# A recurrent layer on one core: half of the odd step's update goes from VectorE to GpSimd, silu is made in one ScalarE instruction, gates by tanh, a shorter layer norm

## The chip, the cores and the metric

One Trainium2 chip; the program uses one of its cores. The metric is the device time in microseconds (us), from one launch to its end; lower is better. All arithmetic is fp32.

## The reference, cut to what matters

x has 8 sequences of 2048 tokens of 512 features. Each token is normalised twice (a plain layer norm `xn`, and a second one with gain and bias inside the layer), goes through a depthwise convolution of three taps along time, and then through matrix products:

```python
x_norm = _layernorm(xn, ln_in_g, ln_in_b)
x_norm = x_norm + conv(x_norm) + conv_b
gate, input_gate = split(x_norm @ gate_w.T + gate_b)
gate = sigmoid(gate)
Bm = x_norm * sigmoid(input_gate) @ B_w.T + B_b
Cm = x_norm @ C_w.T + C_b
A_bar = expm(dt_A * A)                      # 64 x 64
def step(state, bc):                        # 2048 times, state is 8 x 64
    b_t, c_t = bc
    s = _layernorm(state @ A_bar + b_t, ln_st_g, ln_st_b)
    return (s, c_t * s)
ssm = ys @ D_w.T + D_b
out = x + (ssm * gate) * silu(xn @ W.T + b + (xn @ V_r) @ C.T)
```

The scan of 2048 dependent steps on a state of 8 x 64, with a layer norm in each, is what can't be done in parallel.

## The kernel before, in words

**Chunks.** Time is cut into 32 chunks (`NC`) of 64 steps (`CT`). One iteration i of the main loop runs the 64 scan steps of chunk i ("F"), prepares chunk i+1 (layer norm, transposes, convolution, input gate, B and C products: "A"), computes the layer norm statistics of x two chunks ahead ("S"), and finishes chunk i-1 (y, the output product, gating, adding x, storing: "C"). The order on each engine is written out by hand: tables of numbers say behind which scan step t (0 to 63) each piece of side work stands (`V_CONV`, `V_SILU`, `V_SG`, `V_STATS`, `V_XG`, `V_ADD`, `V_G` for VectorE, `PE_...` for TensorE, `POOL_LN` for GpSimd). ScalarE has no scan work; its order is in `iteration` of its block.

**The scan.** Tile `dw` holds, for each of the 8 sequences (partitions) and each step t, a slot of columns: r (`CR`, one), a constant (`CE`), w (`CD` to `CM`, 64), a (`CM` to `CM2`, 64) and a third block (`CM2` to `SLOT`, 64). w is the centred, not yet scaled state; r is 1 over its standard deviation. Steps come in pairs:

- even step (`even_step`): VectorE makes w of t as r(t-1) times a of t-1, added to the slot's w (L727, 64 wide); takes its sum of squares (`square_sum`, L717, into q); then, with the product that TensorE has made from the w of the pair before (`look_ahead`, L990 and L991, in `scanP`), makes a and the third block of t (L731, 128 wide).
- odd step (`odd_step`): VectorE makes w and a of t in one instruction from a and the third block of t-1, scaled by r(t-1) (L740, 128 wide: `CD:CM2` from `CM:SLOT`); takes the sum of squares; transposes w for TensorE (L744).
- behind each sum of squares GpSimd raises q to the power -1/2 and writes r (`step`, L356), and the next step of VectorE waits for it (semaphore `r_ready`).

So a step is: VectorE update, VectorE sum of squares, GpSimd power, and round again. Side work on VectorE stands behind the step's own instructions, while GpSimd makes the power.

**Around it.** silu is made of a sigmoid by ScalarE (`ffn_sigmoid`, L493, tile `sigf`) and two half-wide multiplications by VectorE (`silu`, L679). The input gate (L465) and the output gate (L498) are sigmoids in place in PSUM, each followed by a VectorE product (L673, L686). The layer norm of x is 16 small GpSimd instructions (`ln_op`, L375 to L390): mean negated, variance plus eps, four powers (one column each) for r1, three to get the variance after the first norm, four powers for r2, three products. Each waits for the one before by a semaphore. They stand between the scan's powers, and three groups of them run ahead of the loop. SyncE issues all transfers, x of the next chunks among them (`prefetch_xa`, L246).

Of the kernel before, what the change touches and what calls it, by code (L numbers as in the profile page):

```python
# [13 lines left out]
P = 128  # L14
B = 8
# [63 lines left out]
POOL_LN = (43, 43, 44, 45, 46, 47, 48, 48, 49, 50, 51, 52, 53, 54, 54, 55)  # L79
# [17 lines left out]
def build(nc, x, ident_d, gateT_d, WT_d, VT_d, CrT_d, BT_d, CwT_d, DT_d, vec_d, small_d, Bb_d, out):  # L97
    with ExitStack() as ctx:
# [36 lines left out]
        ln = sb("ln", [P, 8, NJ])  # L135
# [52 lines left out]
        def released(user, i):  # L188
# [157 lines left out]
        def _(pool):  # L346
# [11 lines left out]

            def ln_op(n, k):

                mean, var = mv[:, :, 0], mv[:, :, 1]
                nm, a, r1, v2, r2, rr, bx, bz = (ln[:, a, :] for a in range(8))
# [5 lines left out]
                if k == LN_OPS - 3:  # L368
# [7 lines left out]
                    lambda: g.tensor_scalar(a, var, EPS, None, ALU.add),  # L376
                    lambda: half_power(a, r1, 0),
# [768 lines left out]
```

## Time and profile before

| | |
|---|---|
| median of 3 runs | 2668.4 us (2668.17 to 2672.42) |
| the profiled execution, its own time | 2673.4 us |
| its span in the profile | 2671.6 us |
| VectorE busy | 2163.5 us, 81% |
| GpSimd busy | 1305.1 us, 49% |
| TensorE busy (matmul) | 2510.1 us, 94% |
| ScalarE busy | 826.4 us, 31% |
| granted TensorE clock, mean | 0.991 |

Busy time is the share of the span in which an engine had an instruction under way; the chain of waits follows the work that ended last backwards through whatever released it. The 1.8 us between the profiled execution's time and its span lie outside the span.

### The profile page before, as it was taken

To read this page: it belongs to the slowest core of one execution; us is meant where nothing else is said; L and a number is where in the kernel's file an instruction comes from. 1 tells how busy PE (TensorE), PEld (TensorE's weight loads), DVE (VectorE), ACT (ScalarE), POOL (GpSimd) and SP (SyncE) were. 2 spreads that over 40 slices of the span, in tenths; PEclk is the share of its full clock that TensorE was granted. 3 is DMA by queue.
4 is the path that set the end of the run, shared out by engine and by line. 5 is a ranking of instruction groups with operands and counts; after the bars stand their busy time and mean duration, and the time that the engine had idled before them with its cause. 6 is when DMAs were issued, how large, how long until landed. Compare 5 with 4: busy or idle time off the path is not lost.

```text
span 2671.6 us, 39956 instructions
## 1 busy us (share of the span) xinstructions
PE 2510.1 (94%) x9999; PEld 1303.0 (49%) x9999; DVE 2163.5 (81%) x9732; ACT 826.4 (31%) x1354; POOL 1305.1 (49%) x2584
## 2 busy tenths in 40 slices
PE   2899999999999999999999999999999999999985
PEld 1445555555455555545555545555554555555543
DVE  3478888888888888888888888888888888888875
ACT  0423333322333322333332233332233333223310
POOL 3154455555455555445555545555544555554442
PEclk9999999999999999999999999999999999999997
DMA  2001122112112211211211211221121121121112
GB/s 88 23 22 50 45 51 56 40 38 56 45 47 55 56 39 39 52 45 50 56 42 39 53 47 44 56 56 40 38 54 45 48 56 47 37 50 47 32 36 49
DMA packets 99835, 125.03 MB, mean 47 GB/s; under 512 B 32231, under 2 KB 48807, under 8 KB 99608
## 3 DMA queue, kind: packets, MB, share of 16 engines
q1 hardware_dynamic: 99608, 122.48, 18.3%
q8 instruction: 85, 1.39, 0.2%
q14 instruction: 142, 1.16, 0.1%
HBM read 71.92 MB, written 33.55 MB: 39 GB/s over the span
## 4 chain that ended last, share of the span: by engine, by line
DVE 50%; POOL 34%; issue 12%; PE 3%; POOLq 0%; SPq 0%; ACT 0%; DMA 0%; DVEq 0%; ACTq 0%
POOL dw L356 27%; DVE wq L717 13%; DVE dw L740 11%; DVE dw L727 7%; POOL ln L373 5%; DVE wT L744 4%; DVE bank L658 3%; DVE xnorm L664 3%; DVE sgT L703 3%; DVE xg L673 3%; DVE o L711 1%; DVE G L686 1%; PE bank L957 1%; DVE ys L694 1%; PE bank L897 0%
## 5 line engine op out<-in xcount | busy, mean ns | idle before, releaser
L356 POOL TENSOR_TENSOR dw<-q,minus_half 8x1 f32<-8x1 f32 x2048 | 1105.5, 540 | 1239.7 <-DVE wq L717 1228.3
L990 PEld LDWEIGHTS bank<-Mscan,wT 128*65 128x65 f32 x2046 | 215.8, 136 | 760.1 <-issue 755.3
L740 DVE SCALAR_TENSOR_TENSOR dw<-dw 8x128 f32<-8x128 f32 x1024 | 347.7, 340 | 207.7 <-POOL dw L356 191.1
L957 PE MATMUL bank<-xnorm,gateT 128*128 128x512 f32 x1024 | 508.6, 600 | 0.9 <-issue 0.9
L948 PE MATMUL bank<-xnorm,gateT 128*128 128x512 f32 x1024 | 504.4, 594 | 0.0
L717 DVE SCALAR_TENSOR_TENSOR wq<-dw 8x65 f32<-8x65 f32 x2048 | 443.4, 217 | 70.3
L940 PE MATMUL bank<-xnT,WT 128*128 128x512 f32 x1024 | 494.9, 594 | 0.0
L990 PE MATMUL bank<-Mscan,wT 128*65 128x128 f32 x2046 | 409.9, 282 | 86.6 <-DVE wT L744 36.1
L991 PE MATMUL bank<-Mscan,wT 128*65 128x128 f32 x2046 | 393.0, 274 | 0.0
L727 DVE SCALAR_TENSOR_TENSOR dw<-dw 8x64 f32<-8x64 f32 x1024 | 271.4, 265 | 132.5 <-POOL dw L356 125.6
L731 DVE SCALAR_TENSOR_TENSOR dw<-bank,dw 8x128 f32<-8x128 f32 x1024 | 342.6, 335 | 8.2 <-PE bank L991 7.8
L465 ACT ACTIVATE bank<-bank,vec 128x512 f32<-128x512 f32 x128 | 84.8, 662 | 618.6 <-PE bank L957 618.6
L991 PEld LDWEIGHTS bank<-Mscan,wT 128*65 128x65 f32 x2046 | 254.3, 139 | 0.2
L744 DVE STREAM_TRANSPOSE wT<-dw 32x64 f32<-32x64 f32 x1024 | 232.8, 227 | 0.0
L940 PEld LDWEIGHTS bank<-xnT,WT 128*128 128x128 f32 x1024 | 167.5, 191 | 95.3 <-issue 95.3
L957 PEld LDWEIGHTS bank<-xnorm,gateT 128*128 128x128 f32 x1024 | 161.4, 192 | 90.5 <-issue 89.9
L948 PEld LDWEIGHTS bank<-xnorm,gateT 128*128 128x128 f32 x1024 | 171.1, 191 | 62.1 <-issue 62.1
L498 ACT ACTIVATE bank<-bank,vec 128x512 f32<-128x512 f32 x128 | 84.7, 662 | 374.6 <-PE bank L948 374.6
L493 ACT ACTIVATE sigf<-bank,vec 128x512 f32<-128x512 f32 x128 | 87.6, 684 | 215.1 <-PE bank L940 211.2
L717 DVE DVE_READ_ACCUMULATOR wq<-dw 8x1 f32 x2048 | 145.3, 71 | 0.0
L373 POOL TENSOR_TENSOR ln<-ln,minus_half 128x1 f32<-128x1 f32 x264 | 142.8, 541 | 4.3 <-POOL ln L373 3.2
L920 PE MATMUL bank<-ident,sgT 128*128 128x128 f32 x512 | 141.0, 280 | 1.4 <-DVE sgT L703 0.8
(136 smaller groups left out, 2511.1 us busy)
## 6 DMA issues: line engine op xcount, KB each, us to landing
xa<-in_x SPq DMA_DIRECT2D x256, 128.0 KB, 2.7
xc<-in_x SPq DMA_DIRECT2D x256, 128.0 KB, 2.7
out<-o SPq DMA_DIRECT2D x256, 128.0 KB, 2.3
dw<-dtok SPq DMA_DIRECT2D x128, 96.0 KB
wtok<-dw SPq DMA_DIRECT2D x128, 33.0 KB
gateT<-in_gateT SPq DMA_DIRECT2D x1, 2048.0 KB
WT<-in_WT SPq DMA_DIRECT2D x1, 1024.0 KB, 9.0
xc<-in_x SPq DMA_DIRECT2D x8, 124.0 KB
```

The lines of the kernel that those rows point to most:

```text
L356: nc.gpsimd.tensor_tensor(dw[0:B, t, CR:CR + 1], q[:], minus_half[0:B, 0:1], ALU.pow).then_inc(s["r_ready"], 1)
L373: half_power = lambda a, b, j: g.tensor_tensor(col(b, j), col(a, j), minus_half[:, j:j + 1], ALU.pow)
L717: V.scalar_tensor_tensor(out=wq[:], in0=w_eps, scalar=1.0 / S, in1=w_eps, op0=ALU.mult, op1=ALU.mult, accum_out=q[:]).then_inc(s["q_ready" ...
L727: V.scalar_tensor_tensor(out=dw[0:B, t, CD:CM], in0=dw[0:B, before, CM:CM2], scalar=r, in1=dw[0:B, t, CD:CM], op0=ALU.mult, op1=ALU.add).t ...
L731: V.scalar_tensor_tensor(out=dw[0:B, t, CM:SLOT], in0=scanP[0:B, 0:2 * S], scalar=r, in1=dw[0:B, t, CM:SLOT], op0=ALU.mult, op1=ALU.add).t ...
L740: V.scalar_tensor_tensor(out=dw[0:B, t, CD:CM2], in0=dw[0:B, before, CM:SLOT], scalar=dw[0:B, before, CR:CR + 1], in1=dw[0:B, t, CD:CM2], ...
L744: V.transpose(wT[0:32, 0:S], dw[:, t, CD:CM]).then_inc(s["wT_ready"], 1)
L940: ins = mm(mbank["ffn", m][:], WT[:, k, P * m:P * m + P], xnT[:, k, :], start=(k == 0), stop=(k == KH - 1))
L948: ins = mm(mbank["gate", m][:], gateT[:, k, P * m:P * m + P], xnorm[p][:, k, :], start=(k == 0), stop=(k == KH - 1))
L957: ins = mm(mbank["ig", m][:], gateT[:, k, H + P * m:H + P * m + P], xnorm[p][:, k, :], start=(k == 0), stop=(k == KH - 1))
L990: mm(scanP[0:WIDE, 0:2 * S], wT[:, 0:WIDE], Mscan[:, 0, :], start=True, stop=False)
L991: mm(scanP[0:WIDE, 0:2 * S], wT[:, 32:32 + WIDE], Mscan[:, 1, :], start=False, stop=True).then_inc(s["p_ready"], 1)
```

## The change

1. **The odd step's a goes to GpSimd.** VectorE's odd update is 64 wide now (w alone). GpSimd gets `next_a` ahead of the odd step's power: a multiplication by r(t-1) into a new tile `scaled` (`tensor_scalar`, 8x64) and an addition (`tensor_tensor`, 8x64). The first waits for `r_ready` and `rest_ready`, the second for the first (`a_scaled`). The even step on VectorE waits for `a_ready` too.
2. **silu and gates.** ScalarE makes silu in one instruction straight into `G`; VectorE's eight half-wide products per chunk go. Both gates are tanh of half the argument, and VectorE's products become (tanh + 1) times the other operand; the factors of one half go into `C_b`, `ys`, `BT` and the gates' biases in the setup.
3. **Layer norm.** r1 times r2 is the power -1/2 of var * (1 + EPS) + EPS * EPS, so 13 instructions take the place of 16.
4. **Places.** The statistics stand at t = 18 to 32 instead of 26 to 40, their aggregation at 34 instead of 42, GpSimd's layer norm at 35 to 53 instead of 43 to 55.

```diff
-V_SILU = (6, 8, 12, 14, 16, 18, 20, 22)
-V_STATS = (26, 28, 30, 32, 34, 36, 38, 40)
-V_AGGR = 42
+V_STATS = (18, 20, 22, 24, 26, 28, 30, 32)
+V_AGGR = 34
-POOL_LN = (43, 43, 44, 45, 46, 47, 48, 48, 49, 50, 51, 52, 53, 54, 54, 55)
+POOL_LN = (35, 35, 35, 37, 39, 41, 43, 45, 47, 49, 51, 53, 53)
...
+            def next_a(i, t):
+                here, before = dw[0:B, t, CM:CM2], dw[0:B, t - 1, CM2:SLOT]
+                wait_for(pool, "r_ready", CT, i, t)
+                wait_for(pool, "rest_ready", PAIRS, i, t // 2 + 1)
+                nc.gpsimd.tensor_scalar(scaled[:], before, dw[0:B, t - 1, CR:CR + 1], None,
+                                        ALU.mult).then_inc(s["a_scaled"], 1)
+                wait_for(pool, "a_scaled", PAIRS, i, t // 2 + 1)
+                nc.gpsimd.tensor_tensor(here, scaled[:], here, ALU.add).then_inc(s["a_ready"], 1)
+
             def step(i, t):
+                if t % 2:
+                    next_a(i, t)
                 wait_for(pool, "q_ready", CT, i, t + 1)
...
+                    lambda: g.tensor_scalar(both, var, 1.0 + EPS, EPS * EPS, ALU.mult, ALU.add),
                     lambda: half_power(a, r1, 0),
...
-                    lambda: g.tensor_tensor(v2, var, r1, ALU.mult),
-                    lambda: g.tensor_tensor(v2, v2, r1, ALU.mult),
-                    lambda: g.tensor_scalar(a, v2, EPS, None, ALU.add),
-                    lambda: half_power(a, r2, 0),
...
-                    lambda: g.tensor_tensor(rr, r1, r2, ALU.mult),
+                    lambda: half_power(both, rr, 0),
...
-                a_(mbank["ig", m][:], mbank["ig", m][:], ACT.Sigmoid,
+                a_(mbank["ig", m][:], mbank["ig", m][:], ACT.Tanh, scale=0.5,
...
-            def ffn_sigmoid(c, m):
-                wait_for(act, "silu_done", 2 * KH, c, 2 * m - 2)
-                a_(sigf[:, m % 2, :], mbank["ffn", m][:], ACT.Sigmoid,
-                   bias=v_("ffn_b", m)).then_inc(s["sig_done"], 1)
+            def ffn_silu(c, m, p):
+                if m == 0:
+                    wait_for(act, "sg_done", KH, c - 1, 0)
+                a_(G[p][:, m, :], mbank["ffn", m][:], ACT.Silu, bias=v_("ffn_b", m)).then_inc(s["silu_done"], 1)
...
-                V.tensor_tensor(xg[:, m, :], mbank["ig", m][:], xnorm[p][:, m, :],
-                                ALU.mult).then_inc(s["xg_done"], 1)
-            def silu(c, m, h, p):
-                V.scalar_tensor_tensor(out=G[p][:, m, part], in0=mbank["ffn", m][:, part], scalar=v_("ffn_b", m),
-                                       in1=sigf[:, m % 2, part], op0=ALU.add, op1=ALU.mult
+                V.scalar_tensor_tensor(out=xg[:, m, :], in0=mbank["ig", m][:], scalar=1.0, in1=xnorm[p][:, m, :],
+                                       op0=ALU.add, op1=ALU.mult).then_inc(s["xg_done"], 1)
...
                 wait_for(dve, "r_ready", CT, i, t)
+                wait_for(dve, "a_ready", PAIRS, i, t // 2)
                 V.scalar_tensor_tensor(out=dw[0:B, t, CD:CM], in0=dw[0:B, before, CM:CM2], scalar=r,
...
-                V.scalar_tensor_tensor(out=dw[0:B, t, CD:CM2], in0=dw[0:B, before, CM:SLOT],
-                                       scalar=dw[0:B, before, CR:CR + 1], in1=dw[0:B, t, CD:CM2],
+                V.scalar_tensor_tensor(out=dw[0:B, t, CD:CM], in0=dw[0:B, before, CM:CM2],
+                                       scalar=dw[0:B, before, CR:CR + 1], in1=dw[0:B, t, CD:CM],
...
+            link(V.tensor_scalar(vec[:, gates, :], vec[:, gates, :], 0.5, None, ALU.mult))
+            link(V.tensor_scalar(sm("C_b"), sm("C_b"), 0.5, None, ALU.mult))
```

What stands in a row on GpSimd before, from the start of the loop to the middle of chunk 0 (L356 is the power of a step, L375, L376 and L373 are the first layer norm instructions, behind steps 43 to 45):

```order
L356 TENSOR_TENSOR dw<-q,minus_half 8x1 [waits q_ready] x44
L375 TENSOR_SCALAR ln<-mv 128x4 [waits mv_done,xn_done]
L376 TENSOR_SCALAR ln<-mv 128x4 [waits ln_done]
L356 TENSOR_TENSOR dw<-q,minus_half 8x1 [waits q_ready]
L373 TENSOR_TENSOR ln<-ln,minus_half 128x1 [waits ln_done]
```

And after the change, steps 33 to 38 of a chunk (L367 is the power now, L358 and L361 the two new instructions, L386 to L388 the first three of the layer norm, L384 one of its powers):

```order
L358 TENSOR_SCALAR scaled<-dw 8x64 [waits rest_ready,r_ready]
L361 TENSOR_TENSOR dw<-scaled,dw 8x64 [waits a_scaled]
L367 TENSOR_TENSOR dw<-q,minus_half 8x1 [waits q_ready]
L386 TENSOR_SCALAR ln<-mv 128x4 [waits mv_done,xn_done]
L387 TENSOR_SCALAR ln<-mv 128x4 [waits ln_done]
L388 TENSOR_SCALAR ln<-mv 128x4 [waits ln_done]
L367 TENSOR_TENSOR dw<-q,minus_half 8x1 [waits q_ready]
L358 TENSOR_SCALAR scaled<-dw 8x64 [waits rest_ready,r_ready]
L361 TENSOR_TENSOR dw<-scaled,dw 8x64 [waits a_scaled]
L367 TENSOR_TENSOR dw<-q,minus_half 8x1 [waits q_ready]
L384 TENSOR_TENSOR ln<-ln,minus_half 128x1 [waits ln_done]
```

Between an even step's power and the odd step's power there now stand two instructions, of which the first waits for the even power itself and the second for the first; between an odd power and the next even one stands nothing new but the layer norm's pieces, three of them behind step 35.

VectorE before, steps 26 and 27 with the side work between them (L727 even update, L740 odd update, L717 sum of squares, L744 transpose, L638 statistics):

```order
L727 SCALAR_TENSOR_TENSOR dw<-dw 8x64 [waits r_ready]
L717 SCALAR_TENSOR_TENSOR wq,q<-dw 8x65 [waits w_ready]
L731 SCALAR_TENSOR_TENSOR dw<-bank,dw 8x128 [waits p_ready]
L638 BN_STATS stats<-xa 128x6 [waits xa_in]
L740 SCALAR_TENSOR_TENSOR dw<-dw 8x128 [waits rest_ready,r_ready]
L717 SCALAR_TENSOR_TENSOR wq,q<-dw 8x65 [waits w_ready]
L744 STREAM_TRANSPOSE wT<-dw 32x64
```

VectorE after, a pair of steps with the same kinds of side work (L728 even update, L741 odd update, L645 statistics, L745 transpose):

```order
L728 SCALAR_TENSOR_TENSOR dw<-dw 8x64 [waits a_ready,r_ready]
L717 SCALAR_TENSOR_TENSOR wq,q<-dw 8x65 [waits w_ready]
L732 SCALAR_TENSOR_TENSOR dw<-bank,dw 8x128 [waits p_ready]
L645 BN_STATS stats<-xa 128x6
L741 SCALAR_TENSOR_TENSOR dw<-dw 8x64 [waits rest_ready,r_ready]
L717 SCALAR_TENSOR_TENSOR wq,q<-dw 8x65 [waits w_ready]
L745 STREAM_TRANSPOSE wT<-dw 32x64
```

The odd update has become 64 wide, the even one waits for `a_ready` as well, and the rest stands as it did, less the L679 products that stood behind eight of the even steps.

## Rows read from the trace of the kernel before

**Rows 1.** The page, the chain of waits: shares of the span by engine, then by line.

```profile
DVE 50%; POOL 34%; issue 12%; PE 3%; POOLq 0%; SPq 0%; ACT 0%; DMA 0%; DVEq 0%; ACTq 0%
POOL dw L356 27%; DVE wq L717 13%; DVE dw L740 11%; DVE dw L727 7%; POOL ln L373 5%; DVE wT L744 4%; DVE bank L658 3%; DVE xnorm L664 3%; DVE sgT L703 3%; DVE xg L673 3%; DVE o L711 1%; DVE G L686 1%; PE bank L957 1%; DVE ys L694 1%; PE bank L897 0%
```

**Rows 2.** Timeline, chunk 14: start us, duration us, engine, line, operation [idle before <-releaser].

```profile
1302.00 0.54 POOL L356 TENSOR_TENSOR dw<-q,minus_half 8x1 f32<-8x1 f32 x1 [0.65 <-DVE wq L717]
...
1302.57 0.34 DVE L740 SCALAR_TENSOR_TENSOR dw<-dw 8x128 f32<-8x128 f32 x1 [0.39 <-POOL dw L356]
1302.94 0.22 DVE L717 SCALAR_TENSOR_TENSOR wq<-dw 8x65 f32<-8x65 f32 x1
...
1303.25 0.54 POOL L356 TENSOR_TENSOR dw<-q,minus_half 8x1 f32<-8x1 f32 x1 [0.71 <-DVE wq L717]
...
1303.82 0.27 DVE L727 SCALAR_TENSOR_TENSOR dw<-dw 8x64 f32<-8x64 f32 x1 [0.50 <-POOL dw L356]
...
1304.43 0.54 POOL L356 TENSOR_TENSOR dw<-q,minus_half 8x1 f32<-8x1 f32 x1 [0.65 <-DVE wq L717]
```

**Rows 3.** Timeline of GpSimd: the scan's first power and, 2047 powers on, its last.

```profile
124.12 0.54 POOL L356 TENSOR_TENSOR dw<-q,minus_half 8x1 f32<-8x1 f32 x1 [9.04 <-DVE wq L717]
...
2648.88 0.54 POOL L356 TENSOR_TENSOR dw<-q,minus_half 8x1 f32<-8x1 f32 x1 [0.74 <-DVE wq L717]
```

**Rows 4.** Timeline of VectorE, chunk 0: the longest wait of the scan for TensorE.

```profile
129.05 0.34 DVE L731 SCALAR_TENSOR_TENSOR dw<-bank,dw 8x128 f32<-8x128 f32 x1 [2.58 <-PE bank L991]
```

**Rows 5.** GpSimd, groups of the whole span: count | busy us, mean ns | idle before.

```profile
L348 POOL MEMSET dw<- 32x12416 f32 x1 | 10.4, 10435 | 0.0
L375 POOL TENSOR_SCALAR ln<-mv 128x4 f32<-128x4 f32 x33 | 8.0, 243 | 79.4 <-issue 41.3 <-DVE mv L650 35.6
...
L383 POOL TENSOR_SCALAR ln<-ln 128x4 f32<-128x4 f32 x33 | 7.3, 220 | 0.6 <-POOL ln L382 0.6
L382 POOL TENSOR_TENSOR ln<-ln 128x4 f32<-128x4 f32 x33 | 6.6, 201 | 5.9 <-POOL ln L381 5.9
...
L351 POOL MEMSET dw<- 8x64 f32 x1 | 0.2, 208 | 0.0
...
L350 POOL MEMSET dw<- 8x1 f32 x1 | 0.1, 89 | 0.1
```

**Rows 6.** Timeline of GpSimd, layer norm ahead of the loop, each waiting for the last.

```profile
56.93 0.20 POOL L382 TENSOR_TENSOR ln<-ln 128x4 f32<-128x4 f32 x1 [0.18 <-POOL ln L381]
57.33 0.23 POOL L383 TENSOR_SCALAR ln<-ln 128x4 f32<-128x4 f32 x1 [0.20 <-POOL ln L382]
57.74 0.57 POOL L373 TENSOR_TENSOR ln<-ln,minus_half 128x1 f32<-128x1 f32 x1 [0.18 <-POOL ln L383]
```

**Rows 7.** Timeline of GpSimd, chunk 14: a power of the layer norm behind one of the scan.

```profile
1288.55 0.54 POOL L356 TENSOR_TENSOR dw<-q,minus_half 8x1 f32<-8x1 f32 x1 [0.20 <-DVE wq L717]
1289.07 0.54 POOL L373 TENSOR_TENSOR ln<-ln,minus_half 128x1 f32<-128x1 f32 x1
```

**Rows 8.** VectorE, groups of the whole span.

```profile
L740 DVE SCALAR_TENSOR_TENSOR dw<-dw 8x128 f32<-8x128 f32 x1024 | 347.7, 340 | 207.7 <-POOL dw L356 191.1
...
L727 DVE SCALAR_TENSOR_TENSOR dw<-dw 8x64 f32<-8x64 f32 x1024 | 271.4, 265 | 132.5 <-POOL dw L356 125.6 <-DMA dw<-dtok 6.9
...
L679 DVE SCALAR_TENSOR_TENSOR G<-bank,vec,sigf 128x256 f32<-128x256 f32 x256 | 118.4, 463 | 0.0
```

**Rows 9.** Stretch, busy us (count) of PE, PEld, DVE, ACT, POOL, clock, DMA share, GB/s.

```profile
1230.00:1309.00 79.00, 77.03 (x312) 40.00 (x311) 66.68 (x302) 25.78 (x44) 40.21 (x80) 1.00 0.19 48
```

**Rows 10.** ScalarE: its one table load of the span.

```profile
L515 ACT ACT_TABLE_LOAD x1 | 1.3, 1283 | 0.7 <-PEq L1136 0.7
```

**Rows 11.** Timeline of SyncE, chunk 14: the eight transfers of x for the statistics.

```profile
1242.88 4.95 SPq L246 DMA_DIRECT2D xa<-in_x  x8
```

**Rows 12.** The page, DMA issues: KB each, median us from issue to landing.

```profile
xa<-in_x SPq DMA_DIRECT2D x256, 128.0 KB, 2.7
```

**Rows 13.** Timeline of GpSimd, chunk 14: the power of step 18.

```profile
1253.03 0.54 POOL L356 TENSOR_TENSOR dw<-q,minus_half 8x1 f32<-8x1 f32 x1 [0.70 <-DVE wq L717]
```

More of the change, by code:

```diff
@@ L361, in ln_op @@
                 mean, var = mv[:, :, 0], mv[:, :, 1]
-                nm, a, r1, v2, r2, rr, bx, bz = (ln[:, a, :] for a in range(8))
+                nm, a, r1, both, rr, bx, bz = (ln[:, a, :] for a in range(7))
                 if k == 0:
@@ L380, in ln_op @@
                     lambda: half_power(a, r1, 3),
-                    lambda: g.tensor_tensor(v2, var, r1, ALU.mult),
-                    lambda: g.tensor_tensor(v2, v2, r1, ALU.mult),
-                    lambda: g.tensor_scalar(a, v2, EPS, None, ALU.add),
-                    lambda: half_power(a, r2, 0),
-                    lambda: half_power(a, r2, 1),
-                    lambda: half_power(a, r2, 2),
-                    lambda: half_power(a, r2, 3),
-                    lambda: g.tensor_tensor(rr, r1, r2, ALU.mult),
+                    lambda: half_power(both, rr, 0),
+                    lambda: half_power(both, rr, 1),
+                    lambda: half_power(both, rr, 2),
+                    lambda: half_power(both, rr, 3),
                     lambda: g.tensor_tensor(bx, nm, r1, ALU.mult),
@@ L672, in gated_x @@
                     wait_for(dve, "xnorm_done", KH, c, KH)
-                V.tensor_tensor(xg[:, m, :], mbank["ig", m][:], xnorm[p][:, m, :],
-                                ALU.mult).then_inc(s["xg_done"], 1)
-            def silu(c, m, h, p):
-                wait_for(dve, "sig_done", KH, c, m + 1)
-                part = slice(TOK // 2 * h, TOK // 2 * (h + 1))
-                V.scalar_tensor_tensor(out=G[p][:, m, part], in0=mbank["ffn", m][:, part], scalar=v_("ffn_b", m),
-                                       in1=sigf[:, m % 2, part], op0=ALU.add, op1=ALU.mult
-                                       ).then_inc(s["silu_done"], 1)
+                V.scalar_tensor_tensor(out=xg[:, m, :], in0=mbank["ig", m][:], scalar=1.0, in1=xnorm[p][:, m, :],
+                                       op0=ALU.add, op1=ALU.mult).then_inc(s["xg_done"], 1)
             def whole_gate(c, m, p):
                 wait_for(dve, "gates_done", KH, c, m + 1)
-                wait_for(dve, "silu_done", 2 * KH, c, 2 * m + 2)
-                V.tensor_tensor(G[p][:, m, :], mbank["gate", m][:], G[p][:, m, :],
-                                ALU.mult).then_inc(s["g_done"], 1)
+                wait_for(dve, "silu_done", KH, c, m + 1)
+                V.scalar_tensor_tensor(out=G[p][:, m, :], in0=mbank["gate", m][:], scalar=1.0, in1=G[p][:, m, :],
+                                       op0=ALU.add, op1=ALU.mult).then_inc(s["g_done"], 1)
             def state_times_c(c, p):
@@ L794, in _ @@
                         if n == 1:
-                            ins = V.tensor_scalar(btmp[:], btmp[:], -1.0 / S, None, ALU.mult)
+                            ins = V.tensor_scalar(btmp[:], btmp[:], -0.5 / S, None, ALU.mult)
                         else:
-                            ins = V.tensor_tensor(BT[:, :, 0:S], BT[:, :, 0:S], btmp[:].unsqueeze(2).to_broadcast([P, KH, S]),
-                                                  ALU.add)
+                            ins = V.scalar_tensor_tensor(out=BT[:, :, 0:S], in0=BT[:, :, 0:S], scalar=0.5,
+                                                         in1=btmp[:].unsqueeze(2).to_broadcast([P, KH, S]),
+                                                         op0=ALU.mult, op1=ALU.add)
                     ins.then_inc(s["bt_steps"], 1)
@@ L866, in iteration @@
                     if F:
-                        if t in V_SILU:
-                            silu(i, *divmod(V_SILU.index(t), 2), p)
                         if t in gate_at:
@@ L1101, in _ @@
             iteration(NC, 0, "C", False)
-LN_OPS = 16
-SETUP_VEC = 1
+LN_OPS = 13
+SETUP_VEC = 3
 SETUP_SERIES = SETUP_VEC + 11
```

45 lines of the change are left out of this document (23 added, 22 removed).

## The prediction

> **What bounds the kernel now.** I read the chain of waits first. VectorE has 50% of it and GpSimd 34% [rows 1], and the lines are those of the scan: the power, the sum of squares, the two updates. So the question is not which engine is busiest but how long one round is. The timeline of a calm stretch shows it [rows 2]. A power starts at 1302.00 and takes 0.54; the odd update starts at 1302.57, the sum of squares at 1302.94, the next power at 1303.25: 1.25 us from the even power to the odd one. From there the even update starts at 1303.82 and the next power at 1304.43: 1.18 us. The reader should see that the odd step is 0.07 longer for one reason: its update is 128 wide, 340 ns against 265 ns [rows 8]. In both, VectorE is idle until the power is done (0.39 and 0.50 before the updates).
>
> The first and the last of the 2048 powers are 2524.76 us apart [rows 3]. One wait of 2.58 us for TensorE at the start of chunk 0 is a single event [rows 4]; without it, a pair of steps takes 2 x (2524.76 - 2.58) / 2047 = **2.464 us**, against 1.25 + 1.18 = 2.43 in the calm stretch. The whole kernel is 1024 such pairs, 124 us ahead of them and some 23 behind. VectorE's side work hides in the power's shadow and costs the other 0.03. Hence every 0.01 us in a pair is 10.2 us of time.
>
> **The change, part by part.** *The new path on GpSimd.* Between the even power and the odd one there were 1.25 us, all VectorE's. Now two ways have to be through before the odd power starts, and the longer decides.
>
> VectorE's way: the update is 64 wide as in the even step, so 1.18 us.
>
> GpSimd's way, from the start of the even power: 0.54 for the power; then the multiplication, which waits for that power's result by a semaphore on the same engine; then the addition, which waits for the multiplication; then the power, which does not wait for the addition. What an instruction pays that waits for the one before it on GpSimd is in the layer norm ahead of the loop [rows 6]: 0.20 ahead of a tensor_scalar, 0.18 ahead of a tensor_tensor. One that doesn't wait starts 0.02 before the end of the last (1288.55 to 1289.07 is 0.52 for a power of 0.54) [rows 7]. The way is therefore L = 0.54 + 0.20 + m + 0.18 + s - 0.02 = 0.90 + m + s, with m and s the times of the two instructions.
>
> No row has these on 64 elements. With 4 elements a tensor_scalar takes 0.22 and a tensor_tensor 0.20 [rows 5]. For 60 elements more, the fills give two rates [rows 5]: the large one 10.4 us / 12416 = 0.84 ns per element, the small one on the very shape 8x64 (208 - 89) / 63 = 1.9 ns, though that one is strided. At 0.84 it is m = 0.27, s = 0.25; at 1.9, m = 0.33, s = 0.31; and if each of the addition's two inputs costs 1.9, s = 0.43. I take s = 0.31, since the addition reads two inputs and the fill none, and m = 0.30, between its two ends: its operand is contiguous, but its factor comes from memory, while the factors of the rows are constants. So **L = 1.51**, with ends 1.42 and 1.66. GpSimd's way is longer than VectorE's by 0.33.
>
> The Trainium skill speaks against this move: "GPSIMD Engine Reference", section "Engine selection", gives elementwise adds and multiplies to VectorE, with GpSimd about two times slower on two inputs and at about line rate on one. By its figures (one element per cycle at 1.2 GHz for the multiplication, 4497 ns for 2048 elements for the addition) I estimate m at 0.27 and s at 0.33, and the total would be 10 us less than mine; no row here shows either on 64 elements.
>
> *The gap from the odd power to the even one* stays 1.18. The even update waits for `a_ready` too, but the addition is over before the odd power starts. A second satisfied wait costs nothing: the odd update had two and starts 0.57 behind the power, as the even one does with one [rows 2]. Side work behind odd steps no longer runs over, because VectorE now gets there L - 1.18 = 0.33 before GpSimd starts the power. A pair is 1.51 + 1.18 = 2.69, and 1024 x (2.69 - 2.464) = **+231 us**.
>
> *The layer norm's start.* Behind step 35 stand three dependent tensor_scalars: from the start of the power 0.52, then three of about 0.24 with two gaps of some 0.19, less 0.02: 1.60 instead of 1.18 [rows 5 to 7]. In 30 chunks that is **+12 us**. The other places hold one power, 0.52 + 0.54 = 1.06, or two products, about 1.10, both under 1.18.
>
> *Ahead of the loop.* The layer norm there loses four instructions of some 0.4 from start to start [rows 6] and gains one, -1.1; two more small VectorE instructions in the setup, at about half a microsecond together, +0.5. **-0.6 us**.
>
> *Costed at nothing.* The removed silu products, 256 x 463 ns = 118 us of VectorE [rows 8], lay in the shadow of the even power and ran over it by a few hundredths; that gain is in the 2.464, and it can't appear while GpSimd is later. The same goes for the 75 ns of the narrower update. ScalarE's silu and tanh: it is busy 25.8 of 79 us in a chunk [rows 9]; were silu and tanh in different tables, two loads of 1.28 [rows 10] per chunk would still fit, and the list of instructions holds one load, as before. The gate products with a constant added lie behind odd steps, with 0.33 us more cover than before. The statistics at step 18: x is issued by 1247.83, lands some 2.7 later at 1250.5, and the first statistics would stand behind the power of step 18 at 1253.03 [rows 11 to 13], 2.5 us later; longer steps make it more. TensorE was busy 77.0 of 79 us in a chunk [rows 9] and would be next if pairs got shorter; here they get longer.
>
> Sum: 231 + 12 - 1 = +242. On the profiled execution, 2673.4, that is 2915.9; it is 5 above the median of the runs, so **2911 us**.
>
> **The rivals.** With T(L) = 2668.4 + 11.4 + 1024 x (L + 1.18 - 2.464):
>
> *Cheap elements.* Both instructions at 0.84 ns per element, L = 1.42: **2819 us**. For it: a fill of the same engine runs so. Against: it has no input.
>
> *A shared path to memory.* While GpSimd multiplies and adds, VectorE runs the odd update and the sum of squares, both reading `dw` twice. If GpSimd has to stand back for the elements of one of them, 340 - 265 = 0.075 us [rows 8], or of both, L is 1.585 to 1.66: **2988 to 3065 us**. The two-input end for s comes to 3065 as well. For it: the timing coincides in every pair. Against: nothing in the trace shows GpSimd stretched, but its powers read one element. The Trainium skill, "Advanced Engine Details and Errata", section "GPSIMD Details", has the two engines share a read and a write interface, in conflict when VectorE has two inputs in SBUF; these two instructions have that.
>
> *The other side: VectorE's way decides.* If GpSimd starts its multiplication without the 0.20 and the addition without the 0.18, and both add little for 60 elements, L falls under 1.18. Then the narrower update and the vanished silu products count in full: pairs of 2.36, 1024 x (2.36 - 2.464) = -107, and with the layer norm's 11.4 **2573 us**. It turns at 0.90 + m + s + 1.18 = 2.464 - 0.011, that is m + s = 0.37. The rows have 0.22 + 0.20 = 0.42 with 4 elements already, so this needs the waits to be cheaper than in every one of the rows.
>
> *The change does not do what it says:* GpSimd's two instructions might be off the path if the odd power stood ahead of them. The order shows them ahead of it, so I give this nothing.
>
> **How the numbers follow.** Forecast, L from 1.48 to 1.55 (2880 to 2952): 0.42. Cheap elements, down to 2810: 0.22. Shared path or two-input rate, up to 3070: 0.29; beyond, 0.02. VectorE decides: 0.03. Near the turning point, within 0.2% (5 us, what a measurement can just tell from no change): 0.02. The range takes the cheap case and most of the dear one: 2810 to 3030. Faster 0.03, same 0.02, slower 0.95.
>
> **What would show it.** In the changed kernel's timeline, GpSimd should have no idle time before the odd power that VectorE ended; the even power, the two new instructions and the odd power should stand in a row with 0.20 and 0.18 between them, 1.5 us from power to power, and 1.18 to the next. VectorE's idle time before the even update should grow, and its busy share fall to some 68% (2163 - 118 - 77 of 2914). GpSimd should lead the chain of waits. Idle time of GpSimd ended by the sum of squares ahead of the odd power would say that VectorE's way decides, and make me wrong; new instructions of 0.4 us or more would say that the elements or the shared path are dearer; a long wait of the statistics for x would say that moving them had a price.

## The result, and the profile after

| | before | after |
|---|---|---|
| median | 2670.4 us (4 runs) | 2962.2 us (4 runs, 2961.8 to 2964.5) |
| ratio to before | | 1.1095 (95% interval 1.1075 to 1.1114) |
| span of the profiled execution | 2671.6 us | 2960.5 us |
| VectorE busy | 2163.5 us, 81% | 2058.8 us, 70% |
| GpSimd busy | 1305.1 us, 49% | 2127.4 us, 72% |

The change makes the kernel 291.8 us slower. The chain of waits of the changed kernel, by engine and by line, answers to [rows 1]:

```profile
POOL 68%; DVE 17%; issue 12%; PE 2%; POOLq 0%; SPq 0%; ACT 0%; DVEq 0%; DMA 0%; ACTq 0%
POOL dw L367 37%; POOL scaled L358 18%; POOL dw L361 11%; DVE dw L728 9%; DVE wq L717 7%; PE bank L960 1%; PE bank L900 0%; POOL ln L398 0%; POOLq L219 0%; SPq L255 0%; POOL ln L387 0%; POOL ln L386 0%; PE bank L986 0%; ACT z L432 0%; POOL ln L397 0%
```

GpSimd went from 34% to 68% of the chain, and the two new instructions (L358, L361) are 29% of it. A pair of steps in the timeline of GpSimd and VectorE of the changed kernel, which answers to [rows 2]:

```profile
1399.83 0.54 POOL L367 TENSOR_TENSOR dw<-q,minus_half 8x1 f32<-8x1 f32 x1 [0.70 <-DVE wq L717]
...
1400.40 0.27 DVE L741 SCALAR_TENSOR_TENSOR dw<-dw 8x64 f32<-8x64 f32 x1
1400.47 0.53 POOL L358 TENSOR_SCALAR scaled<-dw 8x64 f32<-8x64 f32 x1
1400.71 0.22 DVE L717 SCALAR_TENSOR_TENSOR wq<-dw 8x65 f32<-8x65 f32 x1
...
1401.08 0.31 POOL L361 TENSOR_TENSOR dw<-scaled,dw 8x64 f32<-8x64 f32 x1
...
1401.35 0.56 POOL L367 TENSOR_TENSOR dw<-q,minus_half 8x1 f32<-8x1 f32 x1
...
1401.94 0.27 DVE L728 SCALAR_TENSOR_TENSOR dw<-dw 8x64 f32<-8x64 f32 x1 [0.27 <-POOL dw L367]
...
1402.56 0.54 POOL L367 TENSOR_TENSOR dw<-q,minus_half 8x1 f32<-8x1 f32 x1 [0.65 <-DVE wq L717]
```

The power of the even step starts at 1399.83, the multiplication at 1400.47, the addition at 1401.08 and the odd power at 1401.35: 1.52 us where there were 1.25. There is no idle time in front of the odd power; VectorE had its sum of squares by 1400.93 (the row at 1400.71 lasts 0.22), 0.42 earlier. From the odd power to the next even one (1402.56) it is 1.21. The groups of the whole span show that this pair is like the others, and answer to [rows 5] and [rows 8]:

```profile
L358 POOL TENSOR_SCALAR scaled<-dw 8x64 f32<-8x64 f32 x1024 | 538.7, 526 | 105.1 <-DVE dw L732 3.9
L361 POOL TENSOR_TENSOR dw<-scaled,dw 8x64 f32<-8x64 f32 x1024 | 315.4, 308 | 85.3
```

```profile
L728 DVE SCALAR_TENSOR_TENSOR dw<-dw 8x64 f32<-8x64 f32 x1024 | 279.9, 273 | 417.5 <-POOL dw L367 410.1 <-DMA dw<-dtok 7.0
L741 DVE SCALAR_TENSOR_TENSOR dw<-dw 8x64 f32<-8x64 f32 x1024 | 279.3, 273 | 322.3 <-POOL dw L367 307.1
```

The multiplication takes 526 ns, much more than any row of before had suggested; the addition takes 308. The first and the last power of the scan (the columns are start, duration):

```profile
123.14 0.54 POOL L367 TENSOR_TENSOR dw<-q,minus_half 8x1 f32<-8x1 f32 x1 [10.26 <-DVE wq L717]
...
2938.07 0.56 POOL L367 TENSOR_TENSOR dw<-q,minus_half 8x1 f32<-8x1 f32 x1
```

They are 2814.93 us apart, against 2524.76 [rows 3]: the scan is 290.2 us longer. The spans of the two profiled executions differ by 288.9, so the whole loss is in the scan, and what lies outside it is 1.3 us shorter. Behind step 35 stand the three dependent layer norm instructions, 1.67 us from power to power:

```profile
1404.08 0.56 POOL L367 TENSOR_TENSOR dw<-q,minus_half 8x1 f32<-8x1 f32 x1
...
1404.63 0.22 POOL L386 TENSOR_SCALAR ln<-mv 128x4 f32<-128x4 f32 x1
...
1405.04 0.24 POOL L387 TENSOR_SCALAR ln<-mv 128x4 f32<-128x4 f32 x1 [0.20 <-POOL ln L386]
...
1405.47 0.20 POOL L388 TENSOR_SCALAR ln<-mv 128x4 f32<-128x4 f32 x1 [0.19 <-POOL ln L387]
...
1405.75 0.56 POOL L367 TENSOR_TENSOR dw<-q,minus_half 8x1 f32<-8x1 f32 x1
```

### The profile page after: what moved, and what is told of

Same layout as the page of the kernel before. It is cut to its first block, busy times and chain, and to the rows that moved or that the text cites. A ratio compares the mean times of both kernels' runs of the same rounds, so it can differ in the third digit from the quotient of the medians.

```text
span 2960.5 us, 43376 instructions
## 1 busy us (share of the span) xinstructions
PE 2575.8 (87%) x9999; PEld 1287.0 (43%) x9999; DVE 2058.8 (70%) x9478; ACT 828.5 (28%) x1354; POOL 2127.4 (72%) x4533
## 4 chain that ended last, share of the span: by engine, by line
POOL 68%; DVE 17%; issue 12%; PE 2%; POOLq 0%; SPq 0%; ACT 0%; DVEq 0%; DMA 0%; ACTq 0%
POOL dw L367 37%; POOL scaled L358 18%; POOL dw L361 11%; DVE dw L728 9%; DVE wq L717 7%; PE bank L960 1%; PE bank L900 0%; POOL ln L398 0%; POOLq L219 0%; SPq L255 0%; POOL ln L387 0%; POOL ln L386 0%; PE bank L986 0%; ACT z L432 0%; POOL ln L397 0%
## 5 line engine op out<-in xcount | busy, mean ns | idle before, releaser
L367 POOL TENSOR_TENSOR dw<-q,minus_half 8x1 f32<-8x1 f32 x2048 | 1122.2, 548 | 518.4 <-DVE wq L717 488.0
L993 PEld LDWEIGHTS bank<-Mscan,wT 128*65 128x65 f32 x2046 | 199.6, 136 | 1064.1 <-issue 1063.6
L358 POOL TENSOR_SCALAR scaled<-dw 8x64 f32<-8x64 f32 x1024 | 538.7, 526 | 105.1 <-DVE dw L732 3.9
L728 DVE SCALAR_TENSOR_TENSOR dw<-dw 8x64 f32<-8x64 f32 x1024 | 279.9, 273 | 417.5 <-POOL dw L367 410.1
L741 DVE SCALAR_TENSOR_TENSOR dw<-dw 8x64 f32<-8x64 f32 x1024 | 279.3, 273 | 322.3 <-POOL dw L367 307.1
L717 DVE SCALAR_TENSOR_TENSOR wq<-dw 8x65 f32<-8x65 f32 x2048 | 451.1, 220 | 70.3
L361 POOL TENSOR_TENSOR dw<-scaled,dw 8x64 f32<-8x64 f32 x1024 | 315.4, 308 | 85.3
L994 PEld LDWEIGHTS bank<-Mscan,wT 128*65 128x65 f32 x2046 | 254.7, 139 | 0.1
L745 DVE STREAM_TRANSPOSE wT<-dw 32x64 f32<-32x64 f32 x1024 | 232.9, 227 | 0.0
L501 ACT ACTIVATE G<-bank,vec 128x512 f32<-128x512 f32 x128 | 87.5, 683 | 240.8 <-PE bank L943 237.0
L384 POOL TENSOR_TENSOR ln<-ln,minus_half 128x1 f32<-128x1 f32 x264 | 142.2, 539 | 4.3 <-POOL ln L384 3.8
```

Source lines behind the costliest of these rows:

```text
L358: nc.gpsimd.tensor_scalar(scaled[:], before, dw[0:B, t - 1, CR:CR + 1], None, ALU.mult).then_inc(s["a_scaled"], 1)
L361: nc.gpsimd.tensor_tensor(here, scaled[:], here, ALU.add).then_inc(s["a_ready"], 1)
L717: V.scalar_tensor_tensor(out=wq[:], in0=w_eps, scalar=1.0 / S, in1=w_eps, op0=ALU.mult, op1=ALU.mult, accum_out=q[:]).then_inc(s["q_ready" ...
L728: V.scalar_tensor_tensor(out=dw[0:B, t, CD:CM], in0=dw[0:B, before, CM:CM2], scalar=r, in1=dw[0:B, t, CD:CM], op0=ALU.mult, op1=ALU.add).t ...
L741: V.scalar_tensor_tensor(out=dw[0:B, t, CD:CM], in0=dw[0:B, before, CM:CM2], scalar=dw[0:B, before, CR:CR + 1], in1=dw[0:B, t, CD:CM], op0 ...
L993: mm(scanP[0:WIDE, 0:2 * S], wT[:, 0:WIDE], Mscan[:, 0, :], start=True, stop=False)
```

## The experiments

Two theories stood at the start. One: GpSimd's way from the even to the odd power is the whole loss, and inside it a multiplication by a factor from memory is dear by itself. The other: VectorE and GpSimd stand in each other's way while both read `dw`. Beside them there was the question of what the other parts of the change give or cost.

### a back on VectorE, all else kept

```diff
-                if t % 2:
-                    next_a(i, t)
...
-                V.scalar_tensor_tensor(out=dw[0:B, t, CD:CM], in0=dw[0:B, before, CM:CM2],
+                V.scalar_tensor_tensor(out=dw[0:B, t, CD:CM2], in0=dw[0:B, before, CM:SLOT],
...
```

> The changed kernel with the odd update's a back on VectorE (128 wide) and nothing of the scan but the power on GpSimd; silu on ScalarE, tanh gates and the shorter layer norm stay. Theory, GpSimd's way alone made the loss: the gap from even to odd power goes from 1.52 back to 1.25 us and the time to 2668 to 2685 us, the 12 or so above the kernel before being the three dependent instructions behind step 35. Rival, the removed silu products were worth something: under 2665. Rival, the new silu, tanh or layer norm cost something of their own: over 2700.

Measured: 2678.3 us, ratio to before 1.0029 (1.0018 to 1.0040). The loss is gone, so it was GpSimd's way. What is left, some 8 us, has its place behind step 35, where the three layer norm instructions keep the next power waiting. These are the powers of steps 35 and 36 in GpSimd's timeline, with the three layer norm instructions between them; step 34's power starts at 1274.06:

```profile
1275.31 0.54 POOL L365 TENSOR_TENSOR dw<-q,minus_half 8x1 f32<-8x1 f32 x1 [0.71 <-DVE wq L715]
...
1276.96 0.56 POOL L365 TENSOR_TENSOR dw<-q,minus_half 8x1 f32<-8x1 f32 x1
```

1.65 us instead of 1.18 in 30 chunks is 14 us, of which the old places' own overruns (0.07 behind step 43, a little elsewhere) give back some. The removed silu products gave nothing: the gaps behind steps 6 to 22 are 1.25 with and without them.

### Only a moved, the rest as before

```diff
+                if t % 2:
+                    next_a(i, t)
...
-                V.scalar_tensor_tensor(out=dw[0:B, t, CD:CM2], in0=dw[0:B, before, CM:SLOT],
+                V.scalar_tensor_tensor(out=dw[0:B, t, CD:CM], in0=dw[0:B, before, CM:CM2],
...
```

> The kernel before with nothing changed but a's multiplication and addition on GpSimd. Theory: a pair of steps as in the changed kernel, 1.52 + 1.20 us, and on top of it the layer norm instructions that stand behind even steps here (four powers and four products per chunk), which now stand between the even power and the multiplication: some 0.5 us for each power less 0.1, about 2.3 us per chunk, 3000 to 3030 us. Rival, VectorE's relief by the silu move hides a part of GpSimd's way in the changed kernel: then the gap is over 1.55 in chunk parts with silu products (steps 6 to 22).

Measured: 3016.3 us, ratio 1.1295 (1.1275 to 1.1315), as expected. The steps with silu products have the same 1.52, so VectorE's relief hides nothing. The layer norm's powers behind even steps do cost: this is step 44's place in GpSimd's timeline, 1.88 us from power to power.

```profile
1442.62 0.56 POOL L369 TENSOR_TENSOR dw<-q,minus_half 8x1 f32<-8x1 f32 x1
1443.15 0.54 POOL L386 TENSOR_TENSOR ln<-ln,minus_half 128x1 f32<-128x1 f32 x1
1443.69 0.45 POOL L360 TENSOR_SCALAR scaled<-dw 8x64 f32<-8x64 f32 x1
1444.22 0.31 POOL L363 TENSOR_TENSOR dw<-scaled,dw 8x64 f32<-8x64 f32 x1
1444.50 0.56 POOL L369 TENSOR_TENSOR dw<-q,minus_half 8x1 f32<-8x1 f32 x1
```

The row at 1443.69 shows something else. The same multiplication (L360 here) takes 0.45 instead of 0.53 when it starts late, with VectorE's odd update over and its sum of squares (1443.52 to 1443.74) all but over. That spoke for the shared path.

### A constant factor, and a tensor_tensor

```diff
-                nc.gpsimd.tensor_scalar(scaled[:], before, dw[0:B, t - 1, CR:CR + 1], None,
+                nc.gpsimd.tensor_scalar(scaled[:], before, 0.5, None,
```

> The changed kernel with the multiplication by a constant 0.5 instead of r from memory: it leaves out the scaling of a by r, so the computed states differ. Theory, the factor from memory makes the multiplication 0.526 us long: it falls to 0.25 to 0.30 and the time by 1024 x 0.23 to 0.27, to 2685 to 2730 us. Rival, VectorE's two-input reads stretch it, or 64 elements do: it stays above 0.45 and the time above 2880.

```diff
-                nc.gpsimd.tensor_scalar(scaled[:], before, dw[0:B, t - 1, CR:CR + 1], None,
-                                        ALU.mult).then_inc(s["a_scaled"], 1)
+                nc.gpsimd.tensor_tensor(scaled[:], before, dw[0:B, t - 1, CR:CR + 1].to_broadcast([B, S]),
+                                        ALU.mult).then_inc(s["a_scaled"], 1)
```

> The changed kernel with the multiplication as a tensor_tensor, r read as a second input that repeats along the row. Theory, the factor of tensor_scalar is what is dear: this takes about 0.31 us like the addition, and the time falls by 1024 x 0.22 = 225 to about 2740 us. Rival, contention: two inputs read by GpSimd against VectorE's two make it as long or longer, 2950 or more.

Measured: 2788.4 and 2888.5 us, one run each. Both missed what the theory gave, 2685 to 2730 and about 2740, and what the rivals gave, over 2880 and 2950 or more; they lie between. The groups of the first:

```profile
L358 POOL TENSOR_SCALAR scaled<-dw 8x64 f32<-8x64 f32 x1024 | 375.6, 367 | 94.1 <-DVE dw L732 4.3
```

```profile
L741 DVE SCALAR_TENSOR_TENSOR dw<-dw 8x64 f32<-8x64 f32 x1024 | 362.9, 354 | 320.3 <-POOL dw L367 305.0
```

The multiplication fell only to 367 ns, and VectorE's odd update rose from 273 to 354. In the second, the timeline of both engines:

```profile
1402.24 0.54 POOL L367 TENSOR_TENSOR dw<-q,minus_half 8x1 f32<-8x1 f32 x1 [0.64 <-DVE wq L717]
...
1402.81 0.40 DVE L741 SCALAR_TENSOR_TENSOR dw<-dw 8x64 f32<-8x64 f32 x1 [0.39 <-POOL dw L367]
1402.85 0.28 POOL L358 TENSOR_TENSOR scaled<-dw 8x64 f32<-8x64 f32 x1
1403.21 0.31 POOL L361 TENSOR_TENSOR dw<-scaled,dw 8x64 f32<-8x64 f32 x1
1403.25 0.36 DVE L717 SCALAR_TENSOR_TENSOR wq<-dw 8x65 f32<-8x65 f32 x1
...
1403.69 0.54 POOL L367 TENSOR_TENSOR dw<-q,minus_half 8x1 f32<-8x1 f32 x1 [0.17 <-DVE wq L717]
```

The multiplication takes 0.28 here, but VectorE's odd update takes 0.40 and its sum of squares 0.36, each stretched while GpSimd has one of its two instructions under way (without them they are 0.27 and 0.22). The odd power at 1403.69 no longer waits for GpSimd's addition, which ended at 1403.52, but for VectorE, so most of what GpSimd won was lost on the other engine. Neither theory alone fits: the factor from memory has a price, and so has the shared path, which can fall on either side.

### The same three, with VectorE kept away

```diff
                 wait_for(dve, "rest_ready", PAIRS, i, t // 2 + 1)
+                wait_for(dve, "a_ready", PAIRS, i, t // 2 + 1)
                 V.scalar_tensor_tensor(out=dw[0:B, t, CD:CM], in0=dw[0:B, before, CM:CM2],
```

> The changed kernel in which VectorE's odd update waits for the addition of its own step as well, so that GpSimd multiplies and adds while VectorE reads nothing of dw. Its time is no measure (some 3500 to 3700 us); the durations are. Theory, the shared path to memory stretches the multiplication: it falls from 0.526 to under 0.40 us. Rival, a factor from memory is dear by itself: it stays at 0.50 or more and the time is near 2962 + 1024 x 0.67 = 3650 us.

> The same with the multiplication by a constant 0.5 (it leaves out the scaling of a by r). Theory of the shared path: from 0.367 to about 0.27 us. Rival: it stays at 0.367, and what a factor from memory costs is the difference to the run with the factor, 0.16 us.

> The same with the multiplication as a tensor_tensor. Theory, GpSimd with two inputs holds the path and VectorE waits: the multiplication stays at 0.28 us, while VectorE's odd update falls from 0.405 back to 0.265 us and its sum of squares from 0.35 to 0.22. Rival, VectorE's instructions are longer for another reason (the scaled tile, the order): they stay over 0.35.

The times are 3682.8, 3591.9 and 3476.7 us, one run each. The multiplication of the first, then of the second, then of the third and VectorE's odd update there (L742):

```profile
L358 POOL TENSOR_SCALAR scaled<-dw 8x64 f32<-8x64 f32 x1024 | 450.6, 440 | 105.2 <-DVE dw L732 3.9
```

```profile
L358 POOL TENSOR_SCALAR scaled<-dw 8x64 f32<-8x64 f32 x1024 | 374.7, 366 | 92.5 <-DVE dw L732 2.5
```

```profile
L358 POOL TENSOR_TENSOR scaled<-dw 8x64 f32<-8x64 f32 x1024 | 289.1, 282 | 84.1 <-DVE dw L732 3.5
```

```profile
L717 DVE SCALAR_TENSOR_TENSOR wq<-dw 8x65 f32<-8x65 f32 x2048 | 443.2, 216 | 71.0
...
L742 DVE SCALAR_TENSOR_TENSOR dw<-dw 8x64 f32<-8x64 f32 x1024 | 279.1, 273 | 1189.6 <-POOL dw L361 1189.6
```

With the factor from memory the multiplication is 440 ns alone and 526 beside VectorE. With a constant it is 366 both ways; with a tensor_tensor 282 both ways, and there VectorE's odd update is back at 273 and its sum of squares at 216. So the 526 are made of three parts: **366 for 64 elements by a constant, 74 for the factor from memory, 86 for the shared path**. The 366 of the constant hide a price as well, only it is VectorE that pays it beside them (354 instead of 273). Both expectations for the first run missed: it lies between under 400 and 500 or more. The second run went the rival's way: the length of this form, not the path, keeps it at 366; but the 0.16 us that the rival gave the factor are 0.074, the rest is the path. The third went the theory's way.

Who has to wait is not settled by who starts first. In the changed kernel VectorE's odd update starts at 1400.40 and the multiplication 0.07 later, and GpSimd is stretched; with the tensor_tensor the update starts at 1402.81 and the multiplication 0.04 later, and VectorE is. The order in which the two read was not seen, only the starts and the lengths, so the reason stays open.

The third run shows one thing more. The groups of the power in the first and in the third:

```profile
L367 POOL TENSOR_TENSOR dw<-q,minus_half 8x1 f32<-8x1 f32 x2048 | 1122.1, 548 | 1294.5 <-DVE wq L717 1264.1
```

```profile
L367 POOL TENSOR_TENSOR dw<-q,minus_half 8x1 f32<-8x1 f32 x2048 | 1101.5, 538 | 1299.8 <-DVE wq L717 1269.5
```

The mean of 548 is made of 538 at even steps and 558 at odd ones. With the tensor_tensor both are 538. In both runs the odd power follows the addition after 0.74 us of idle time, so its 0.02 us more in the changed kernel go with the tensor_scalar two instructions before it, and not with following the addition directly; why, no run shows.

### The gap between dependent instructions

The prediction put 0.20 and 0.18 between them; the changed kernel has 0.10 and 0.08. The layer norm's instructions, from which the numbers came, have a semaphore increment (`hold`) between the wait and the work, and the two new ones have none.

```diff
+                hold(pool)
                 nc.gpsimd.tensor_scalar(scaled[:], before, dw[0:B, t - 1, CR:CR + 1], None,
...
+                hold(pool)
                 nc.gpsimd.tensor_tensor(here, scaled[:], here, ALU.add).then_inc(s["a_ready"], 1)
```

> The changed kernel with one more instruction of GpSimd's sequencer, the semaphore increment that the layer norm's instructions have between wait and work (hold), ahead of the multiplication and of the addition. Theory: the 0.18 to 0.20 between dependent layer norm instructions holds this increment, and the new pair has 0.10 and 0.08 because it has none; with it the two gaps become 0.18 to 0.20, and the time rises by 1024 x 0.2 = 205 to about 3170 us. Rival, the gap depends on the size or kind of the work: the gaps stay near 0.09, time 2960 to 2990.

Measured: 3122.0 us, one run. GpSimd's timeline (here L359 is the multiplication, L363 the addition, L369 the power):

```profile
1402.59 0.54 POOL L369 TENSOR_TENSOR dw<-q,minus_half 8x1 f32<-8x1 f32 x1 [0.18 <-DVE wq L719]
1403.36 0.44 POOL L359 TENSOR_SCALAR scaled<-dw 8x64 f32<-8x64 f32 x1 [0.23 <-POOL dw L369]
1403.98 0.31 POOL L363 TENSOR_TENSOR dw<-scaled,dw 8x64 f32<-8x64 f32 x1 [0.18 <-POOL scaled L359]
1404.26 0.56 POOL L369 TENSOR_TENSOR dw<-q,minus_half 8x1 f32<-8x1 f32 x1
```

The gaps are 0.23 and 0.18 now, as the theory said. The time is below the expected 3170 because the multiplication, starting 0.14 later, meets only the end of VectorE's update and takes 0.44, its length alone. Now it is VectorE's sum of squares that is stretched:

```profile
L719 DVE SCALAR_TENSOR_TENSOR wq<-dw 8x65 f32<-8x65 f32 x2048 | 498.1, 243 | 70.3
```

That is 216 ns at even steps and 270 at odd ones, off the path here. So the same form of the multiplication is stretched at one moment and stretches VectorE at another. For the time: gaps plus 0.24, length minus 0.09 is 0.15, times 1024 is 154 us; 160 were measured.

### Two versions that keep a on VectorE

The first run leaves the places where a round runs over. This one starts from it and moves three things, and the statistics two steps later, ahead of the layer norm (`V_CONV` counts half taps now, of four sequences each; a gate product of the next version is halved in the same way):

```diff
-V_CONV = (3, 5, 7, 9, 11, 13, 17, 19)
+V_CONV = (3, 4, 5, 6, 7, 8, 9, 10, 11, 12, 13, 14, 16, 17, 18, 19)
-POOL_LN = (35, 35, 35, 37, 39, 41, 43, 45, 47, 49, 51, 53, 53)
+POOL_LN = tuple(range(37, 50))
-V_STATS = (18, 20, 22, 24, 26, 28, 30, 32)
-V_AGGR = 34
+V_STATS = (20, 22, 24, 26, 28, 30, 32, 34)
+V_AGGR = 36
...
                         (odd_step if t % 2 else even_step)(i, t)
+                        if (t + 1) % QT == 0 and (t < CT - 1 or A):
+                            wait_for(dve, D_IN[(t + 1) // QT % NQ], 16, i + (t + 1) // CT, 16)
...
```

> The kernel of the first run (a on VectorE, silu on ScalarE) with three things moved: the layer norm's 13 instructions one behind each power from step 37 to 49, the convolution's taps in halves over the steps 3 to 19, and VectorE's wait for the scan's inputs a step earlier, behind the odd step's transpose. Theory, a round is bound by its longest way and each of these ran over by 0.06 us (eight odd steps with whole taps, four steps with the extra wait) or 0.47 (step 35): every even gap 1.25, every odd one 1.18, 2670 - 32 = 2635 to 2650 us, faster than both kernels. Rival, the gaps of 1.24 behind steps 3 to 19 come from something else than the length of the taps: 2660 to 2672.

Measured: 2644.4 us, ratio to before 0.9907 (0.9890 to 0.9923), faster than both kernels and within what was expected. Odd gaps with half taps behind them are 1.18, and so are those behind steps 15, 31, 47 and 63, in which the wait for the scan's inputs had stood. In GpSimd's timeline it was 1.25 us from the power of step 15 to the next in the first run, and is 1.19 here:

```profile
1250.74 0.54 POOL L365 TENSOR_TENSOR dw<-q,minus_half 8x1 f32<-8x1 f32 x1 [0.71 <-DVE wq L715]
1251.99 0.54 POOL L365 TENSOR_TENSOR dw<-q,minus_half 8x1 f32<-8x1 f32 x1 [0.71 <-DVE wq L715]
```

```profile
1233.63 0.54 POOL L365 TENSOR_TENSOR dw<-q,minus_half 8x1 f32<-8x1 f32 x1 [0.71 <-DVE wq L721]
1234.82 0.54 POOL L365 TENSOR_TENSOR dw<-q,minus_half 8x1 f32<-8x1 f32 x1 [0.65 <-DVE wq L721]
```

The second version takes a out of the odd update on VectorE itself, in ten steps of a chunk:

```diff
+V_SPLIT = (1, 31, 45, 49, 51, 53, 55, 57, 59, 63)
+V_G = (50, 52, 54, 56, 58, 60, 61, 62)
...
+                split = t in V_SPLIT
+                one = slice(CD, CM) if split else slice(CD, CM2)
+                two = slice(CM, CM2) if split else slice(CM, SLOT)
...
                 V.transpose(wT[0:32, 0:S], dw[:, t, CD:CM]).then_inc(s["wT_ready"], 1)
+                if split:
+                    V.scalar_tensor_tensor(out=dw[0:B, t, CM:CM2], in0=dw[0:B, before, CM2:SLOT],
+                                           scalar=dw[0:B, before, CR:CR + 1], in1=dw[0:B, t, CM:CM2],
+                                           op0=ALU.mult, op1=ALU.add).then_inc(s["a_ready"], 1)
```

> The kernel of e8 with, in ten odd steps of a chunk that have no whole side product behind them (1, 31, 45, 49 to 59, 63), a taken out of VectorE's odd update into an instruction of its own behind the transpose, in the shadow of the odd power; the output gate's products stand in halves, mostly behind even steps. Theory: what the changed kernel wanted, the narrow update on the path, is to be had on VectorE itself: in those ten steps the gap from even to odd power falls from 1.25 to 1.18 and the one behind them stays 1.18, 32 x 10 x 0.07 = 22 us off, 2618 to 2628 us. Rival, the instruction behind the transpose does not fit into the 0.5 us and lengthens the next gap by as much: 2640 to 2650.

Measured: **2626.7 us, ratio 0.9833 (0.9819 to 0.9846)**, 45 us faster than the kernel before. VectorE's timeline at a split step: the narrow update L754, the sum of squares L725, the transpose L758, and a on its own, L760.

```profile
1399.74 0.27 DVE L754 SCALAR_TENSOR_TENSOR dw<-dw 8x64 f32<-8x64 f32 x1
1400.05 0.22 DVE L725 SCALAR_TENSOR_TENSOR wq<-dw 8x65 f32<-8x65 f32 x1
...
1400.20 0.23 DVE L758 STREAM_TRANSPOSE wT<-dw 32x64 f32<-32x64 f32 x1
1400.36 0.24 DVE L760 SCALAR_TENSOR_TENSOR dw<-dw 8x64 f32<-8x64 f32 x1
1400.92 0.27 DVE L738 SCALAR_TENSOR_TENSOR dw<-dw 8x64 f32<-8x64 f32 x1 [0.32 <-POOL dw L366]
```

It takes 0.24 and VectorE still waits 0.32 for the power behind it. The chain of waits of this kernel no longer begins with VectorE or GpSimd, as it does before (DVE 50%), after (POOL 68%) and in the version before this one (DVE 43%, POOL 40%):

```profile
PE 85%; DVE 5%; issue 4%; POOL 4%; SPq 0%; ACT 0%; DMA 0%; POOLq 0%; DVEq 0%; ACTq 0%
```

TensorE is busy 95% of the span, and at one of the ten places it already decides. Behind step 54 VectorE's instruction that takes TensorE's product (L742) starts late:

```profile
1273.24 0.34 DVE L742 SCALAR_TENSOR_TENSOR dw<-bank,dw 8x128 f32<-8x128 f32 x1 [0.17 <-PE bank L1016]
```

The half gate product behind it then holds up the narrow update, and from the power of step 54 to that of step 55 it is 1.30 us instead of 1.18. At the other nine the gap is 1.18 to 1.19, as the theory said: 9 x 0.065 x 32 = 19 us less, and some 1.5 more at step 54. The scan is 16.8 us shorter than in the version before, and the medians differ by 18, against 22 worked out.

## Why the prediction was right

The forecast was 2911 us, slower; 2962.2 was measured, inside the range and on the forecast side, though just above the likeliest case (2880 to 2952), in that of the shared path. What bounds the kernel and which way decides were right; that the number for GpSimd's way came out is luck, since two errors in its terms cancel.

- **What bounds the kernel.** Right. The time moved by 1024 times what a pair moved by, and 118 us of VectorE work removed with silu, and 67 ns less in each odd update, bought nothing. GpSimd leads the chain and VectorE's idle time before the even update grew, as foretold; VectorE's busy share is 70% where 68 was worked out.
- **GpSimd's way, L.** 1.51 forecast, 1.52 measured, but the terms were wrong in two places and made up for each other. The multiplication m was put at 0.30, between 0.27 and 0.33, and is 0.53: the factor from memory (74 ns) and the shared path (86 ns) were left out of it, and even with a constant it takes 366 ns, 36 more than the upper end. So m is 0.23 too small. The two gaps were put at 0.20 and 0.18 and are 0.10 and 0.08, 0.20 too large together, because the rows they came from hold one more instruction each. The addition, 0.31 forecast, is 0.308.
- **The gap behind the odd power.** 1.18 forecast, 1.20 measured, and 1.26 at four steps of a chunk. This is where most of the missing 51 us are: 0.02 x 1024 = 20 us, since the odd power takes 0.56 instead of 0.54, which goes with the tensor_scalar; 3 for 1.183 rounded to 1.18; 4 x 0.06 x 32 = 8 us for the wait for the scan's inputs, which the forecast did not name (it was in the 2.464, and I took it for side work); and 1.5 at the place behind step 35, which costs 1.67 - 1.20 = 0.47 instead of 0.42. Another 14 are the hundredth and a half by which L was short. The last 5 are those that the forecast took off because the profiled execution of before lay that much above the median; that of the changed kernel lies at its median.
- **"A second satisfied wait costs nothing."** Held: the even update starts 0.03 behind the power's end as before (from 1401.35 + 0.56 to 1401.94). Not every wait is free, though: the one for the scan's inputs, ahead of the others in four steps of a chunk, costs 0.06, with one other wait in the first run and with two here, and nothing once it stands a step earlier.
- **The rival of the shared path.** It was true, at about its lower price: 86 ns on GpSimd where 75 was worked out, with hardly anything on VectorE's side in the changed kernel (its odd sum of squares 224 instead of 216). The forecast had set it aside as a rival, and only the gaps, 0.20 too large, kept the total near. The page it named, "Advanced Engine Details and Errata" of the Trainium skill, agrees with the runs beside and apart: 526 against 440 ns, and 405 against 273.
- **The Trainium skill on one input at line rate** ("GPSIMD Engine Reference", "Engine selection") led to the estimate m = 0.27; measured are 0.366 with a constant, so at 64 elements this did not hold. The estimate for the addition from the same page's figures, 0.33 against 0.308 measured, was near.
- **Costed at nothing.** Statistics, silu, tanh and the gate products did cost nothing: with a back on VectorE the kernel is 8 us from the one before, and the layer norm's start (14 us, less what its old places had cost) explains that.

## What to carry to other kernels

In a loop of dependent steps, work moved to a helper engine is only free if the whole of that engine's way (its own waits included) is shorter than what the other engine still has to do; here it had 0.64 us and needed 0.98. Look first for the shadow on the same engine: the same update, done by VectorE behind its transpose, cost nothing at nine of ten places. The form of the helper's instruction counts too: a tensor_tensor in place of the tensor_scalar took 74 us off (2888.5, one run), far from enough. And when two errors are possible in opposite directions, check each term, since a sum that comes out right shows neither.

## What the runs showed of the hardware

- GpSimd and VectorE, both on operands in SBUF, stretched each other: the 8x64 multiplication 440 to 526 ns, VectorE's 64-wide update 273 to 405 and its sum of squares 216 to 356. Which one was stretched depended on the form of the GpSimd instruction and on when it started (the same multiplication, 0.14 us later, stayed at 440 while VectorE's sum of squares went from 216 to 270).
- On GpSimd a tensor_tensor with a repeated operand (282 ns) was faster than a tensor_scalar with a constant (366) or with a factor from memory (440), on the same 8x64.
- One more sequencer instruction between a wait on the engine's own result and the work cost 0.11 and 0.14 us on GpSimd.
- The power behind the multiplication and the addition took 558 ns where the multiplication was a tensor_scalar and 538 where it was a tensor_tensor.
- A satisfied wait for a transfer ahead of VectorE's even update cost 0.06 us; a step earlier it cost nothing.
- A 128x512 silu straight from PSUM took 683 ns on ScalarE, the sigmoid in its place before 684.
